# A gated cross-attention block with a feed-forward part: first feed-forward product by Strassen's scheme, in alternation with the second

## The reference

```python
x = x + tanh(g_xattn) * xattn(layernorm(x), ctx)      # 8 heads of 64, softmax over 750 keys
x = x + tanh(g_ffn) * ffn(layernorm(x))
# ffn, with E = 8, D = 512, H = 1024:
h = gelu(einsum('nd,edh->neh', xf, w1) + b1)           # first product
y = einsum('neh,ehd->ned', h, w2) + b2                 # second product
out = (y * norm_g[:, None, None]).sum(axis=1)          # one gate value per token, from xf @ gate_w.T
```

## Time and profile before

| | us |
|---|---|
| median of three runs | 1983.69 (1983.63 to 1985.01) |
| span of the profiled execution | 1982.4 |
| PE busy | 1918.0 (97%) |
| PEld busy | 1719.5 (87%) |
| DVE busy | 903.9 (46%) |
| ACT busy | 780.1 (39%) |
| POOL busy | 237.8 (12%) |
| PE's share of the chain that ended last, `bank` and `scores` products | 31% and 30% |
| DMA moved | 84.01 MB, mean 42 GB/s |

### The profile page before, as it was taken

How to read it: one execution, slowest core, us unless ns; L and a number is a source line. 1 busy time by engine, 2 the same in 40 slices (tenths; PEclk the granted TensorE clock), 3 DMA queues, 4 the chain that set the end, 5 groups by cost and what they waited for, 6 DMA issues and landing times.

```text
span 1982.4 us, 30405 instructions
## 1 busy us (share of the span) xinstructions
PE 1918.0 (97%) x10933; PEld 1719.5 (87%) x10933; DVE 903.9 (46%) x1621; ACT 780.1 (39%) x1532; POOL 237.8 (12%) x194
## 2 busy tenths in 40 slices
PE   4999999999999988999999999999999999999999
PEld 4999999999999977898898898898898898888888
DVE  3677777777777764233124124124115114214232
ACT  3676766767666641222222232222223213212231
POOL 3223232323323231000000000000000000000000
PEclk9999999999999988999999999999999999999999
DMA  5002021110201052002002002002002002002021
GB/s 160 16 22 74 11 73 32 45 57 21 72 19 48 29 201 93 1 22 64 0 1 84 0 0 85 0 0 85 0 0 77 8 0 74 11 0 70 4 78 61
DMA packets 53836, 84.01 MB, mean 42 GB/s; under 512 B 20192, under 2 KB 22304, under 8 KB 53792
## 3 DMA queue, kind: packets, MB, share of 16 engines
q1 hardware_dynamic: 53792, 83.42, 13.5%
HBM read 68.72 MB, written 14.68 MB: 42 GB/s over the span
## 4 chain that ended last, share of the span: by engine, by line
PE 61%; DVE 1%; issue 0%; ACT 0%; DVEq 0%
PE bank L494 31%; PE scores L494 30%; PE scores L681 0%; DVE w2s L865 0%; DVE w2s L722 0%; DVE hs L722 0%; PE bank L691 0%; DVE x_tile L954 0%; DVE acc L892 0%; ACT hs L1066 0%; DVEq L894 0%; DVEq L891 0%
## 5 line engine op out<-in xcount | busy, mean ns | idle before, releaser
L494 PE MATMUL bank<-w2s,hs 128*128 128x512 f32 x2688 | 619.7, 391 | 4.9 <-DVE w2s L722 2.5
L494 PE MATMUL scores<-xT,w1s 128*128 128x384 f32 (+1 forms) x3072 | 621.2, 362 | 1.0 <-DVE w1s L722 1.0
L494 PEld LDWEIGHTS scores<-xT,w1s 128*128 128x128 f32 x3072 | 555.1, 188 | 62.7 <-DVE w1s L722 1.2
L494 PEld LDWEIGHTS bank<-w2s,hs 128*128 128x128 f32 x2688 | 506.4, 189 | 111.2 <-DVE w2s L722 5.8
L1065 ACT ACTIVATE h_full<-scores,b1T 128x512 f32<-128x512 f32 (+1 forms) x256 | 162.5, 635 | 883.1 <-PE scores L494 876.4
L722 DVE TENSOR_TENSOR hs<-h_full,hs 128x512 fp32r<-128x512 f32 (+1 forms) x256 | 161.3, 630 | 426.5 <-ACT hs L1066 425.7
L892 DVE TENSOR_TENSOR acc<-bank,acc 128x512 f32<-128x512 f32 x112 | 77.4, 691 | 426.1 <-PE bank L494 426.1
L1129 POOL TENSOR_SCALAR probs<-probs,row_inv 112x750 f32<-112x750 f32 x64 | 139.6, 2181 | 249.6 <-DVE row_inv L816 249.6
L1066 ACT ACTIVATE hs<-scores,b1T 128x512 fp32r<-128x512 f32 (+1 forms) x256 | 160.7, 628 | 0.0
L494 PE MATMUL bank<-ctxT,wk 128*128 128x376 f32 (+1 forms) x768 | 147.6, 342 | 8.4 <-DVE ctxT L722 7.5
L494 PE MATMUL bank<-wv,ctxT 128*125 128x256 f32 x1152 | 152.7, 283 | 2.9 <-DVE queries L791 2.9
(11 more groups left out here) (98 smaller groups left out, 1336.2 us busy)
## 6 DMA issues: line engine op xcount, KB each, us to landing
w_stage<-in_L_ffn_w SPq DMA_DIRECT2D x64, 512.0 KB, 3.5
ctx_raw<-in_ctx SPq DMA_DIRECT2D x48, 250.0 KB
xt_scratch<-yT SPq DMA_DIRECT2D x32, 224.0 KB, 3.1
xT<-xt_scratch SPq DMA_DIRECT2D x4, 1024.0 KB, 9.0
xa<-in_x SPq DMA_DIRECT2D x16, 224.0 KB, 3.8
xres<-in_x SPq DMA_DIRECT2D x16, 224.0 KB, 2.7
x_scratch<-xres SPq DMA_DIRECT2D x16, 224.0 KB, 2.3
x_tile<-x_scratch SPq DMA_DIRECT2D x14, 256.0 KB, 2.6
```

Of the source, the lines that this page charges most:

```text
L494: mm = pe.matmul(bank, s[i], m[j], start=first and n == 0, stop=last and n == total - 1)
```

## The change

The attention batches but the last keep their order (the plan is written out as text, the items are the same), except that Y now keeps the transposed float32 rows and no low part is made. The last batch and the tail become one hand-written list, `END_PLAN`.

The feed-forward part is rewritten. The tokens are taken in two passes of 896. A step (pass, expert, j) covers 128 hidden units of each half of the hidden width, so there are 2 x 8 x 4 = 64 steps. In a step the first product is a 2x2 block product (448 tokens x 256 of the width x 128 hidden units per block), made by the Winograd form of Strassen's scheme: seven products `P1` to `P7` instead of eight, each of six matmuls of 448 columns. Their inputs are sums of blocks: of the tokens (`xs`, made once per pass: POOL sums, ACT rounds, DVE subtracts) and of the weights (made per step: POOL makes four sums, ACT rounds, POOL subtracts). The results are put together by seven DVE additions (`h_sums`), with one ACT copy (`keep_p1`). Four blocks then go through gelu (twice on ACT) and the low part (`h_low` on DVE). The second product of the step before is made in the same step: after each `P` one 128-token tile of six matmuls of 512 columns (`second`), which DVE adds to `acc`; it now sums over two hidden slices only, so there are four times as many additions. ACT rounds the second weights, and POOL subtracts. The weights are laid out by the caller so that each piece is one DMA of contiguous 4 KB rows.

```diff
-CHUNKS = [(0, 4), (4, 4), (8, 3), (11, 3)]
+NP = 2
+PT = TT // NP
+TH = PT * P // 2
+JS = HT // 2
+MIX = ["P1", "P6", "P2", "P7", "P5", "P4", "P3"]
+BANK_OF = {"P1": 0, "P6": 1, "P2": 2, "P7": 1, "P5": 0, "P4": 2, "P3": 1}
+SUMS = ["U2", "C11", "U3", "C22", "V", "C21", "C12"]
...
+            def product(g, i):
...
+                for kc in range(2):
+                    for s, m in ((0, 0), (0, 1), (1, 0)):
+                        mm = pe.matmul(mb[BANK_OF[name]][:, 0:TH], w1s[j % 2][:, s, W_OF[name], kc, :],
+                                       xs[:, i, m, kc, :], start=n == 0, stop=n == 5)
...
+            def second(g, t):
+
+                p, e, j = g
+                if t == 0:
+                    pe.wait_ge(w2_split, upto(1, g, 1))
+                    pe.wait_ge(h_split, upto(4, g, 3))
+                if t == 3:
+                    pe.wait_ge(h_split, upto(4, g, 4))
...
+                for i in range(NM):
+                    product(g, i)
+                    second(before, i)
+                    if isinstance(e, int) and e == NE - 1 and j == 1 and i in (0, 2, 4):
+                        gate(p, i // 2)
...
+            def sums(g, i):
+                p, e, j = g
+                before = previous(g)
+                for name in {1: ("U2",), 2: ("C11",), 3: ("U3",), 4: ("C22", "V"), 5: ("C21",), 6: ("C12",)}.get(i, ()):
+                    h_sums(g, name)
+                if i == 6:
+                    h_low(g, 2)
+                if before:
+                    add_up(before, i)
+                for q in {3: (0,), 5: (1,), 6: (3,)}.get(i, ()):
+                    h_low(g, q)
...
+            def hidden(g, i):
+                after = following(g)
+                if i == 1 and after and not at(g, (0, 0, 0)):
+                    round_w1(after, 0)
+                if i == 3 and after and not at(g, (0, 0, 0)):
+                    round_w1(after, 1)
+                if i == (6 if at(g, (0, 0, 0)) else 3):
+                    round_w2(g)
+                if i == 0:
+                    keep_p1(g)
+                if i in (2, 4, 5, 6):
+                    gelu(g, (2, 4, 5, 6).index(i))
...
+                after = following(g)
+                if after and not at(g, (0, 0, 0)):
+                    for k in range(5):
+                        w1_part(after, k)
+                split_w2(g)
...
+                if closing and p == 0 and j < 2:
+                    for k in (2 * j, 2 * j + 1):
+                        mix_x(1, k)
```

More of the change, by code:

```diff
@@ L402, in batch @@
                         store_yT(b - 1, qt)
+                    if name == "last" and qt == 0:
+                        load_first()
                     if name != "last":
@@ L483, in _ @@
+            steps(sp, step, (0, 0, 1))
+            for k in range(PT):
+                store_out(1, k)
             for i in range(2):
@@ L699, in _, with step @@
+            def step(g):
+                p, e, j = g
+                before = previous(g)
[4 more added lines that the diff above has]
+                        gate(p, i // 2)
+            steps(pe, step, (0, 0, 1))
+            for t in range(NM):
+                second((NP - 1, NE - 1, JS - 1), t)
         @block.vector
@@ L912, in _ @@
-            e = NE - 1
-            step = [1]
             def chain(ins):
                 ins.then_inc(gate_step, 1)
-                step[0] += 1
-                dve.wait_ge(gate_step, step[0])
-            for k in range(CHUNKS[0][1]):
-                add_up(e, k)
-            dve.wait_ge(gate_tr, 4)
-            dve.wait_ge(scale_loaded, 32)
-            pair = ps[2][:, 0:TT * 16].rearrange("p (t n) -> p t n", t=TT)
-            chain(dve.tensor_copy(logits_tmp[:, :, :], pair[:, :, NE:2 * NE]))
@@ new lines, in split_gate, with step @@
+            def split_gate():
+                dve.wait_ge(small_loaded, 48)
+                dve.wait_ge(small_set, 2)
+                dve.tensor_copy(gate_st[:, :, 0:NE], gate_raw[:, :, :]).then_inc(gate_split, 1)
+                dve.wait_ge(gate_split, 1)
+                sub(gate_st[:, :, NE:2 * NE], gate_raw[:, :, :], gate_st[:, :, 0:NE]).then_inc(gate_split, 1)
+            def step(g):
+                p, e, j = g
+                closing = isinstance(e, int) and e == NE - 1
+                if at(g, (0, 0, 3)):
+                    split_gate()
+                for i in range(NM):
+                    if at(g, (1, 0, 0)) and i < 3:
+                        split_x(1, i + 4)
+                    sums(g, i)
+                    if closing and j == 2 and i in (0, 2, 6):
+                        gate(p, (0, 2, 6).index(i))
+                    if closing and p == 0 and j == JS - 1 and 0 < i < 5:
+                        split_x(1, i - 1)
+                    if at(g, (1, 0, 0)) and i in (2, 4, 6):
+                        result(0, i // 2 - 1)
+                    if at(g, (1, 0, 1)) and i % 2 == 0:
+                        result(0, 3 + i // 2)
@@ L972, in _ @@
+            steps(dve, step, (0, 0, 1))
+            for t in range(NM):
+                add_up((NP - 1, NE - 1, JS - 1), t)
+                result(1, t)
         @block.scalar
```

839 lines of the change are left out of this document (496 added, 343 removed), and 21 rows, old and new, of tables (FILL, HEAD_PLAN, NORMS).

## The result

The changed kernel takes 1953.93 us (median of 4 runs, 1951.35 to 1956.79) against 1983.97 (1983.63 to 1985.01): a ratio of 0.9846, 95% interval 0.9832 to 0.986. The prediction said 1903 us, range 1886 to 1936. The change makes the kernel faster, by 30 us (1.5%, clear of noise) instead of 81. The profiled execution took 1951.35 us, its span is 1949.6.

The account below looks back on a forecast made before the run. PE was taken to bound the feed-forward part: 1982.4 - 77.0 + 1.6 + 4 + 2 + 0.5 - 12 = 1901.5 us of span; the median lies 1.3 above, 1903 us, range 1886 to 1936.

Parts of the forecast that it names:

- The fewer columns of the first product: First product on PE: 2688 matmuls of 448 columns at 0.2002 us take 538.1 instead of 615.1, removing 77.0 us.
- A step of 17.95 us: Steady feed-forward step on PE: 42 x 0.2002 + 42 x 0.2271 = 17.95 us, 2.56 for a product and a tile.
- Changing the group after six matmuls I price at nothing: Feed-forward matmuls on PE: 896 group changes cost nothing, upper end under 6 us.
- DVE and POOL in each other's way: Steady step: low parts on DVE wait for POOL; priced at nothing, at most 1.37 us a step.
- (a): Feed-forward steps: small stalls in every step or costly groups, 0.2 to 0.6 us a step, 1916 to 1941 us; chance 0.21.
- (c): Steady steps: critical low part meets a 2.37 us POOL operation every step, 1.37 us each, 1991 us; chance 0.04.
- The turn, -12 us: Passage from attention to feed-forward: idle time and lower clock partly go, saving 12 us, bounds nothing or all 23.
- 1.6 (gate): Gate on PE: 40 matmuls of 448 columns instead of 32, 8.0 us instead of 6.43, so 1.6 us more.
- 0.5 (tail): End of the kernel: the last seven tiles run alone while DVE adds, 0.5 us more.
- Attention keeps its order: Attention part: a dropped subtraction per transposed tile is off PE's path; nothing (-3 to 0).
- Once per pass, 4 + 2 us: Pass change: extra DVE subtractions and results cost 4 us (0 to 12); the gate coming twice costs 2 (0 to 6).
- (b): Turn and pass change at their bad ends: 12 us not saved, 8 more at pass change; 1923 us, chance 0.10.

Follow-up runs that it names:

- the run with pairs: Against the changed kernel, PE takes two products, then two tiles of the second product, instead of one and one: 1949.18 us, ratio 0.9813.

## Why the prediction was wrong

The direction and the main mechanism were right, and the amount was off by 48.1 us of span (1949.6 against 1901.5). By its steps:

**The fewer columns of the first product: right.** A product of six matmuls of 448 columns takes 1.21 us, the prediction had 1.20. PE bounds the steady part with no idle time.

**A step of 17.95 us: the size was off.** It takes 18.15; over 64 steps that is 12.8 us. The step that failed is "Changing the group after six matmuls I price at nothing", with its upper end of 6 us (896 groups at 0.007 are 6.3). I took it from groups of 12 and 24 matmuls of the same product, which change a bank and a tile; none of them alternates between the two products, and the one with fewer changes was the dearer, so that they showed no cost of a change at all. The alternation costs 0.02 us each time (the run with pairs: 18.15 to 18.09), 0.14 of the 0.20 in a step. The product takes 1.213 instead of 1.201 (0.08 in a step), which is the line between 384 and 512 columns for 448; why it lies above the line no run tests. And 512 columns cost 0.2267 instead of 0.2271, which gives 0.02 back.

**DVE and POOL in each other's way: right, and harmless in a steady step.** The low parts take 1.08 us, above the 0.63, while sums keep 0.62, as forecast. POOL is busy 276.65 us in 470 [stretch above], that is 10.7 in a step, not 9.5, and DVE 12.8, not 11.7. In the steady step from 893.3 us the first low part is the stalled one (at 904.38, 1.74 us, beside POOL's `w1s` from 903.24); the third, which the next step's tile waits for, ends near 911.3, 1.3 us before that tile starts. So neither engine moved a steady step, and rivals (a) and (c), as far as they put stalls into every step, are out. Rival (a)'s other half, "groups that cost", is what happened in part: 0.2 us a step was its lower end.

**The turn, -12 us: wrong in sign.** With the other terms as measured the turn comes out as 1949.6 - 1982.4 + 64.2 (the PE terms) - 1.6 (gate) - 17.8 (once per pass) - 0.5 (tail) = +11.5 us, an error of 23.5. These differences hold the turn as what is left, so small terms that were not measured are in it. The step that failed is "those behind the last head [...] lose their cause and those inside the heads do not", together with "DVE loses four weight splits there, so it is about even": I summed busy times and took from the wait list only what would go. What came is in the profile: POOL at 24.49 us of 29, waits of PE in the heads of 3.44, 2.69, 1.90 and 2.52 us, and a clock of 0.77 where it was 0.93. Inside the heads PE's waits doubled (6.0 to 12.4 us), and behind the last head only 2.0 of 7.5 us went. The bounds "nothing saved, or all 23" left out a loss, though the row of POOL going from 23.6 to 39 us was there. The runs show of its parts: the order of the work nothing (the first tile at 764.9 in the changed kernel, at 765.2 with the old order), the sums 1.7 us, sums and subtractions together 5.2. Of the other 18 us some 4 stand ahead of P2, by the bank that the last batch's first item takes; the prediction had "Attention keeps its order", at "nothing (-3 to 0)", and the bank count wasn't in it. No run alters the count, so how much of the 4 would reach the first tile isn't shown. Some 14 us are not taken apart, and their cause stays open: the roundings on ScalarE, the first weights on GpSimd, the clock behind the gaps, and how much of the 12 us was there to be saved at all.

**Once per pass, 4 + 2 us: 17.8.** That is 16.7 and 1.07 for the first step (19.22 from its second product on). The terms "I take 4 us" and the gate's 2 were too small. Named and shown: DVE's wait for `x` through two buffers, 6.5 us, which the prediction didn't have (it counted "results of 0.7" and not what they wait for); the subtractions at the pass change, 2.3 us of PE's wait; the table loads, 1.4 us for each pair where nothing takes it back. These make some 10 of the 17.8; the rest is not taken apart. This is rival (b)'s second half ("8 more at the pass change") with 12.

So costly groups, a turn nearly twice as bad as rival (b)'s 12 us, and a pass change worse than its 8 came together: 12.8 + 23.5 + 11.8 = 48.1. I had treated these as alternatives with chances of their own, though they are terms that add up, and no rival held two of them but (b).

## What to carry to other kernels

Before giving a full engine new work in a stage with gaps, list for each of its operations on the critical chain what will stand ahead of it in the queue; a sum of busy times below the span says nothing there, and each gap it opens on PE may cost a stretch at the lower clock besides. A price of nothing needs a row that does the same thing: groups that follow each other in one product say nothing of two products in alternation. And a result that is added late wants its operands' whole way looked at, store and load included. Where buffers are given out by counting a list, one item more or less in that list moves a wait to another place: here the first item of a batch, 2.3 us, in a part of the work that had not been changed.

## What was not expected of the hardware

The same stream of matmuls ran at two speeds, both at granted clock 1.00. PE's chain in the run without sums of tokens:

```profile
902.65 1.40 PE bank L687 x6
904.05 1.22 PE scores L662 x6
905.27 1.40 PE bank L687 x6
906.66 1.23 PE scores L662 x6
```

A step takes 18.34 us there instead of 18.15, in all of pass one; behind PE's first wait near 1277 us it is 18.15. The run with sums left out and low parts copied (in the new order) did the same (profiled at 1954.13 us, while other runs of that kernel took down to 1943.4). Over a pass of 28 steady steps it makes 5.3 us. What sets it stays open: it was seen in two profiled runs of fifteen, and in neither of the two of the changed kernel itself. Both leave the sums of tokens out; the third profiled run that does, with the old order, had 18.15.

The second: the wait of 2.3 us near 657, of the same length in all runs, is followed in some runs by a stretch at the lower of the two clock levels and in others not, and the time differs by 2 us.
